# First-norm statistics as sums and centred squares on ScalarE, with the groups of three engines reordered

## The reference

```
mod = silu(c) @ wmod                      # six rows per batch: sa, ca, ga, sb, cb, gb
h   = layernorm(x) * (1 + ca) + sa        # THE FIRST NORM: mean and variance over 512 channels
z   = layernorm(h) * gamma + beta         # second norm, inside the attention block
k, v, r = z @ Wk, z @ Wv, z @ Wr
wkv = tf * kv + td * (decayed running sum of kv over the tokens before)
x   = x + ga * ((sigmoid(r) * wkv) @ Wo)
h   = layernorm(x) * (1 + cb) + sb        # third norm
x   = x + gb * (moe0(h) + moe1(h)) / 2    # two groups of 32 experts, top 2, SwiGLU, dropless
```

## Time and profile before

| | |
|---|---|
| runs | 4863.53, 4865.57, 4850.79 us |
| the profiled execution's own time | 4859.97 us |
| its span, first to last instruction | 4858.2 us |
| PE busy over the span | 4561.6 us (94%) |
| DVE busy | 3056.9 us (63%) |
| ACT busy | 1655.1 us (34%) |
| POOL busy | 2856.0 us (59%) |
| mean granted TensorE clock | 0.974 |

### The profile page before, as it was taken

How to read it: one execution, slowest core, us unless ns; L and a number is a source line. 1 busy time by engine, 2 the same in 40 slices (tenths; PEclk the granted TensorE clock), 3 DMA queues, 4 the chain that set the end, 5 groups by cost and what they waited for, 6 DMA issues and landing times.

```text
span 4858.2 us, 89097 instructions
## 1 busy us (share of the span) xinstructions
PE 4561.6 (94%) x22649; PEld 3757.8 (77%) x22649; DVE 3056.9 (63%) x6077; ACT 1655.1 (34%) x4221; POOL 2856.0 (59%) x2303
## 2 busy tenths in 40 slices
PE   6999999999999993989999998999999999999998
PEld 4878778787878773877777777888788888888886
DVE  5999999999999994444444444544344444444443
ACT  2445444444444441322222222332222222222222
POOL 2677777777777775444545454555455555555554
PEclk8999999999999996999999999999999999999999
DMA  6767676766767676899999989998998988998887
GB/s 242 237 202 241 200 227 207 219 218 210 230 200 223 203 231 206 231 285 255 260 284 269 286 243 285 273 291 201 296 243 233 248 232 229 266 239 222 210 216 193
DMA packets 434618, 1152.40 MB, mean 237 GB/s; under 512 B 59362, under 2 KB 59363, under 8 KB 415667
## 3 DMA queue, kind: packets, MB, share of 16 engines
q0 software_dynamic: 182512, 454.27, 40.3%
q1 hardware_dynamic: 231106, 619.79, 37.7%
q10 hardware_dynamic: 20736, 75.51, 4.2%
HBM read 719.35 MB, written 463.57 MB: 243 GB/s over the span
## 4 chain that ended last, share of the span: by engine, by line
PE 45%; DMA 11%; issue 3%; POOL 1%; DVE 1%; POOLq 0%; SPq 0%; DVEq 0%; ACT 0%
PE ps L1321 13%; PE ps L1323 13%; PE ps L1322 13%; DMA out<-c_yo,c_idx 10%; PE ps L1330 4%; PE ps L1349 2%; DMA c_wt<-wsp_d 1%; POOL out L1312 1%; POOL c_xg L1279 0%; DVE c_yo L1576 0%; POOL list_d L1284 0%; POOLq L1304 0%; DMA list_d<-pairs,sidx 0%; DMA c_lists<-list_d,c_rowu 0%; DVE c_xl L1564 0%
## 5 line engine op out<-in xcount | busy, mean ns | idle before, releaser
L1312 POOL DMA_INDIRECT out<-c_yo,c_idx x576 | 914.8, 1588 | 928.3 <-DMA out<-c_yo,c_idx 475.9
L1321 PE MATMUL ps<-c_wt,c_xh 128*128 128x512 f32 x2304 | 965.6, 419 | 22.6 <-issue 15.1
L1323 PE MATMUL ps<-c_wt,c_xl 128*128 128x512 f32 x2304 | 910.7, 395 | 0.0
L1322 PE MATMUL ps<-c_wt,c_xh 128*128 128x512 f32 x2304 | 904.8, 393 | 0.0
L1279 POOL DMA_INDIRECT c_xg<-h2g_d,c_idx x576 | 566.4, 983 | 519.8 <-DVE c_yo L1576 413.5
L1560 DVE TENSOR_TENSOR c_hh<-ps,c_sil 128x256 f32<-128x256 f32 x576 | 244.4, 424 | 913.7 <-ACT c_sil L1403 849.0
L1576 DVE SCALAR_TENSOR_TENSOR c_yo<-ps,c_wc,c_xg 128x512 f32<-128x512 f32 x576 | 432.5, 751 | 538.7 <-DMA out<-c_yo,c_idx 266.5
L1408 ACT CAST c_xh<-ps 128x512 fp32r<-128x512 f32 x576 | 339.3, 589 | 972.9 <-PE ps L1330 911.7
L711 POOL DMA_INDIRECT list_d<-pairs,sidx x496 | 547.6, 1104 | 186.1 <-issue 124.8
L444 PE MATMUL ps<-xTh,wTh 128*128 128x512 f32 x1536 | 621.5, 405 | 34.5 <-DVE xTl L820 16.8
L1403 ACT ACTIVATE c_sil<-ps 128x256 f32<-128x256 f32 x576 | 221.5, 384 | 1175.2 <-PE ps L1323 1125.0
(11 more groups left out here) (203 smaller groups left out, 7753.4 us busy)
## 6 DMA issues: line engine op xcount, KB each, us to landing
c_wt<-wsp_d SPq DMA_DIRECT2D x69, 2048.0 KB
sraw<-wex SPq DMA_DIRECT2D x290, 256.0 KB
wsp_d<-shigh SPq DMA_DIRECT2D x288, 256.0 KB
wsp_d<-sraw SPq DMA_DIRECT2D x288, 256.0 KB
c_wt<-wsp_d SPq DMA_DIRECT2D x69, 1024.0 KB
xin<-x SPq DMA_DIRECT2D x34, 1024.0 KB
h2g_d<-mod_d SPq DMA_DIRECT2D x128, 256.0 KB
out<-xin SPq DMA_DIRECT2D x32, 1024.0 KB
```

Source lines behind the costliest of these rows:

```text
L1312: nc.gpsimd.indirect_dma_start(out=out, out_offset=bass.IndirectOffsetOnAxis(ap=idx[:, n:n + 1], axis=0), in_=yo[:, n % 4, :], in_offset=N ...
L1321: nc.tensor.matmul(o, lh, rh, start=first, stop=False)
L1322: nc.tensor.matmul(o, lh, rl, start=False, stop=False)
L1323: return nc.tensor.matmul(o, ll, rh, start=False, stop=last)
```

## The change

The DVE statistics of the first norm leave the steps (they stay for the first two tiles, which are done before the loop). ACT computes them instead, in three new groups:

- `sums`: for each of the four j, an Identity activation over 512 channels with an accumulator output, giving the sum. The full-size output goes to a junk buffer, for which `hit` (a buffer of the router code) is lent.
- `mean`: one small Copy that scales the four sums by -1/512 into `fnm`.
- `squares`: for each j, a Square activation with bias `fnm` and an accumulator output, giving the centred sum of squares. A last small activation scales by 1/512 and adds epsilon into `vaf`.

Each of these activations waits for the one before it, since all share the junk buffer. DVE's part 1 adds `fnm` instead of subtracting the mean. The lent buffer brings waits between `sums` and DVE's `place`, and between `squares` and DVE's `topk`. Besides that the order of calls in the step functions of ACT, POOL and DVE is changed. The core of the diff:

```diff
@@ stage_out on SP: the same wait, written through gate()
-                wait(sp, low_of(j), lows(b, j))
+                gate(sp, (low_of(j), lows(b, j)))
@@ ACT, new groups
+            def sums(b, s, js):
+                u = (s + 2) % 4
+                junk = hit[:].rearrange("p k r e -> p (k r e)")
+                if js[0] == 0:
+                    n = (s + 2) // 4 + 1
+                    act.wait_ge(x_in[u], 16 * (b + n) if isinstance(b, int) else b * 16 + n * 16)
+                    wait(act, f_mean, cnt(b, s - 1, 1, 1))
+                    wait(act, at_sum, cnt(b, s - 2, 1, 1))
...
+                for j in js:
+                    wait(act, f_sq, cnt(b, s - 1, 4, 4))
+                    wait(act, f_sum, cnt(b, s, 4, j))
+                    nc.scalar.activation(junk, xin[:, u, j, :], ACT.Identity,
+                                         accum_out=fsum[:, j:j + 1]).then_inc(f_sum, 1)
+
+            def mean(b, s):
+                act.wait_ge(f_sum, cnt(b, s, 4, 4))
+                wait(act, f_sq, cnt(b, s - 1, 4, 4))
+                wait(act, h_half, cnt(b, s + 1, 4, 4))
+                nc.scalar.activation(fnm[:], fsum[:], ACT.Copy, scale=-1.0 / C).then_inc(f_mean, 1)
+
+            def squares(b, s, js):
...
+                for j in js:
+                    act.wait_ge(f_mean, cnt(b, s, 1, 1))
+                    wait(act, f_var, cnt(b, s + 1, 1, 1))
+                    wait(act, f_sq, cnt(b, s, 4, j))
+                    nc.scalar.activation(junk, xin[:, u, j, :], ACT.Square, bias=fnm[:, j:j + 1],
+                                         accum_out=fsq[:, j:j + 1]).then_inc(f_sq, 1)
+                if js[-1] == TJ - 1:
+                    act.wait_ge(f_sq, cnt(b, s, 4, 4))
+                    wait(act, f_rstd, cnt(b, s + 1, 1, 1))
+                    nc.scalar.activation(vaf[:], fsq[:], ACT.Identity, bias=epsc[:], scale=1.0 / C).then_inc(f_var, 1)
@@ ACT step, second half (the first half is in the order rows below)
                 normed(b, s)
-                stage_hi(b, at + 4)
-                chunk_k(b, s, 1)
+                chunk_k(b, s, 2)
                 stage_hi(b, at + 5)
-                chunk_r(b, s, 1)
-                chunk_k(b, s, 2)
+                squares(b, s, (2, 3))
+                stage_hi(b, at + 6)
                 if back_too:
                     turned(b, s)
+                chunk_k(b, s, 3)
                 hi(b, s, 1)
-                stage_hi(b, at + 6)
                 chunk_r(b, s, 2)
-                chunk_k(b, s, 3)
+                stage_hi(b, at + 7)
+                front(b, s, (0, 1))
+                stage_hi(b, at + 8)
+                front(b, s, (2, 3))
+                chunk_r(b, s, 3)
                 hi(b, s, 2)
-                stage_hi(b, at + 7)
-                stage_hi(b, at + 8)
                 stage_hi(b, at + 9)
-                front(b, s, (0, 1))
-                chunk_r(b, s, 3)
-                front(b, s, (2, 3))
                 hi(b, s, 3)
@@ POOL step, around rstd of the third norm
                 stage_lo(b, at + 2)
-                stage_lo(b, at + 3)
                 if not (first and s == 0):
                     rstd(b_var, vab, h2_ready, rsb, b_rstd, b, s - 1)
+                stage_lo(b, at + 3)
                 if old:
-                    scatter(b, s - 2, 0, 7)
+                    scatter(b, s - 2, 0, 6)
+                lo(b, s, 0)
...
@@ DVE, norm_front part 1
+                               scalar=mvf[:, j, 0:1] if early else fnm[:, j:j + 1], in1=mod[:, CA1, :],
+                               op0=ALU.subtract if early else ALU.add, op1=ALU.mult).then_inc(h_half, 1)
@@ DVE, topk, before it writes hit
+                    wait(dve, f_sq, cnt(b, s + 1, 4, 4))
@@ DVE step
-                norm_front(b, s + 1, 3)
                 if not (first and s < 2):
                     place(b, s - 2)
+                norm_front(b, s + 1, 3)
                 if not (first and s == 0):
                     modulate(b, s - 1)
+                chunk(b, s, 1)
+                chunk(b, s, 2)
                 stage_lo(b, s * PER_STEP + 4)
-                chunk(b, s, 1)
                 stage_lo(b, s * PER_STEP + 5)
-                chunk(b, s, 2)
                 stage_lo(b, s * PER_STEP + 6)
-                norm_front(b, s + 2, 0)
                 chunk(b, s, 3)
```

More of the change, by code:

```diff
@@ L260, in stage_a @@
         f_stats, f_aggr, f_var = sem("f_stats"), sem("f_aggr"), sem("f_var")
+        f_sum, f_mean, f_sq = sem("f_sum"), sem("f_mean"), sem("f_sq")
         h_half, h_ready = sem("h_half"), sem("h_ready")
@@ L620, in step @@
                 at = s * PER_STEP
+                stage_hi(b, at)
                 chunk_k(b, s, 0)
-                stage_hi(b, at)
                 stage_hi(b, at + 1)
@@ L626, in step @@
                     soften(b, s - 2)
+                chunk_r(b, s, 1)
+                stage_hi(b, at + 2)
                 hi(b, s, 0)
-                stage_hi(b, at + 2)
                 stage_hi(b, at + 3)
+                chunk_k(b, s, 1)
+                sums(b, s, (0, 1))
+                sums(b, s, (2, 3))
+                mean(b, s)
+                squares(b, s, (0, 1))
+                stage_hi(b, at + 4)
                 normed(b, s)
-                stage_hi(b, at + 4)
-                chunk_k(b, s, 1)
+                chunk_k(b, s, 2)
                 stage_hi(b, at + 5)
-                chunk_r(b, s, 1)
-                chunk_k(b, s, 2)
+                squares(b, s, (2, 3))
+                stage_hi(b, at + 6)
                 if back_too:
                     turned(b, s)
+                chunk_k(b, s, 3)
                 hi(b, s, 1)
-                stage_hi(b, at + 6)
                 chunk_r(b, s, 2)
-                chunk_k(b, s, 3)
+                stage_hi(b, at + 7)
[3 more added lines that the diff above has]
+                chunk_r(b, s, 3)
                 hi(b, s, 2)
-                stage_hi(b, at + 7)
-                stage_hi(b, at + 8)
                 stage_hi(b, at + 9)
-                front(b, s, (0, 1))
-                chunk_r(b, s, 3)
-                front(b, s, (2, 3))
                 hi(b, s, 3)
@@ L717, in step @@
                 at = s * PER_STEP
+                if not (first and s < 3):
+                    scatter(b, s - 3, 11, 13)
                 rstd(f_var, vaf, h_ready, rsf, f_rstd, b, s + 1)
+                stage_lo(b, at)
                 if not (first and s < 3):
-                    scatter(b, s - 3, 11, 16)
-                stage_lo(b, at)
+                    scatter(b, s - 3, 13, 15)
                 receive(b, s, 0)
                 stage_lo(b, at + 1)
-                lo(b, s, 0)
+                if not (first and s < 3):
+                    scatter(b, s - 3, 15, 16)
                 rstd(g_var, vag, z_ready, rsg, g_rstd, b, s + 1)
                 stage_lo(b, at + 2)
-                stage_lo(b, at + 3)
                 if not (first and s == 0):
                     rstd(b_var, vab, h2_ready, rsb, b_rstd, b, s - 1)
+                stage_lo(b, at + 3)
                 if old:
-                    scatter(b, s - 2, 0, 7)
+                    scatter(b, s - 2, 0, 6)
+                lo(b, s, 0)
+                if old:
+                    scatter(b, s - 2, 6, 8)
                 receive(b, s, 1)
                 if old:
-                    scatter(b, s - 2, 7, 8)
+                    scatter(b, s - 2, 8, 9)
                 lo(b, s, 1)
+                stage_lo(b, at + 7)
+                if old:
+                    scatter(b, s - 2, 9, 10)
                 receive(b, s, 2)
-                if old:
-                    scatter(b, s - 2, 8, 9)
-                lo(b, s, 2)
-                stage_lo(b, at + 7)
                 stage_lo(b, at + 8)
                 if old:
-                    scatter(b, s - 2, 9, 10)
+                    scatter(b, s - 2, 10, 11)
+                receive(b, s, 3)
                 stage_lo(b, at + 9)
-                receive(b, s, 3)
-                if old:
-                    scatter(b, s - 2, 10, 11)
+                lo(b, s, 2)
                 lo(b, s, 3)
@@ L904, in topk @@
                 wait(dve, at_sum, cnt(b, s - 1, 1, 1))
-                if isinstance(b, int) and b == 0 and s == 0:
-                    dve.wait_ge(zeroed, 96)
+                if not (isinstance(b, int) and b == B and s == -1):
+                    wait(dve, f_sq, cnt(b, s + 1, 4, 4))
                 V.tensor_tensor(hit[:], iota[:].unsqueeze(1).unsqueeze(1).to_broadcast([P, 2, R, E]),
@@ L1039, in _ @@
             g.memset(half[:], -0.5)
+            g.memset(A["epsc"][:], EPS)
             for t in (A["mvf"], A["mvg"], A["mvb"]):
```

10 lines of the change are left out of this document (8 added, 2 removed).

## The result

The changed kernel is slower: 4984.59 us (median of four runs, 4977.53 to 4997.03) against 4860.98 for the kernel before (4850.79 to 4865.57), a ratio of 1.0263 with an interval of 1.0245 to 1.0282. The forecast was 4924. The profiled execution took 4997.03 with a span of 4995.3, 137 us more than the one before it.

A forecast was written before the change was run, and what follows sets the result against it. It took PE's second third of `project` 3, waiting for DVE's chunk 2 scan, to set stage A's step. Waits 51 plus clock 22 less 9 gave 64 us on 4859.97: 4924 us, own range 4880 to 4965, whole range 4850 to 5000.

The forecast's parts named there:

- the head of ACT's new list: `chunk_r` 1 on ACT, which waits for `project` 1 to end, so the list before `chunk_k` 2 cannot begin earlier.
- 28.55: Offset in us from the step's start at which ACT's list was to begin, after `project` 1.
- 40.65: Offset where ACT's `chunk_k` 2 was to end: 28.55 plus 6.9 us of existing work and 5.2 of new activations.
- 43.6: Offset where PE's second third of `project` 3 was to begin, behind DVE's scan of chunk 2; between 42.3 and 44.5.
- first third done, with `back` hardly waiting: PE was to reach the end of `project` 3's first third at some 41.0, then stop once per step for 2.6 us.
- Waits: Later second third of `project` 3, 6.4 us per batch (51 in all), less 1.1 (9) for the wait ahead of `project` 0.
- Clock: Slow PE clock after its stop in `project` 3: half of 1.4 us per step, 22 us in all, bounds 0 and 45.
- The wait at `back` is nearly gone: Sign at PE's `back`: its wait, mostly for the scan of chunk 1, 25.0 us before, was to nearly vanish.
- The other sign: DVE was to idle before chunk 2 for ACT's `chunk_k`, PE waiting 2 to 3 us within `project` 3.
- Rival 1: On ACT, accumulating activations are cheap and no clock is lost: no change, 4860 us; chance 0.14.
- rival 3: DVE's relief decides if ACT's list does not gate chunk 2: faster, 4775 us, or 4818 for half; chance 0.14.
- Rival 2: Late `stage_lo` 4 holds the staging ring, so `front` 2 and 3 come late and `project` 0 stalls: 5004 us; chance 0.18.

The follow-up runs named there:

- Experiment 2: Changed kernel with the eight accumulating activations reading 4 of 512 channels: 4983.0 us, ratio 1.0258 to the kernel before.
- experiment 1: All three engines' new orders, but statistics left on DVE and nothing new on ACT: 4980.5 us, ratio 1.0257 to the kernel before.
- experiment 3: Changed kernel with `chunk_r` 1 moved from the head of ACT's list to directly behind `chunk_k` 1: 4931.1 us, ratio 1.0155 to the kernel before.
- experiment 10: experiment 3 with DVE's `stage_lo` 4 and 5 back ahead of chunks 1 and 2: 4883.2 us, ratio 1.0079 to the kernel before.
- experiment 4: Changed kernel with `topk` ahead of DVE's first pass (`norm_front` part 1): 4960.7 us, ratio 1.0203 to the kernel before.
- experiment 6: Kernel before with DVE's new order alone, its statistics kept on DVE: 4912.5 us, ratio 1.0132 to the kernel before.
- experiment 12: 11 with DVE's chunk 1 ahead of `stage_lo` 4: 4833.9 us, ratio 0.9970 to the kernel before.
- 8: Kernel before, all orders kept, with the statistics on ACT where it waited: 4860.8 us, ratio 1.0028 to the kernel before.
- 11: 8 with `front` moved ahead of `stage_hi` 8 and 9 on ACT, POOL rearranged accordingly: 4838.9 us, ratio 0.9981 to the kernel before.

## Why the prediction was right or wrong

**The direction was right, the place was wrong.** Slower was forecast at 0.72, and the head of ACT's new list was named for it. That 4984.59 lies above the forecast's own 4880 to 4965 but inside the whole range, 4850 to 5000, is luck: the upper end came from bounds on other terms. The head of the list does wait for `project` 1: `chunk_r` 1 starts at 866.41, offset 28.3 against the 28.55 used. ACT's list then went almost as worked out. The timeline of ACT after:

```profile
870.40 0.63 ACT L634 ACTIVATE hit<-xin 128x512 f32<-128x512 f32 x1 [1.07 <-issue]
870.94 0.18 ACT L634 ACTIVATION_READ_ACCUMULATOR hit<-xin 128x1 f32 x1
871.22 0.63 ACT L634 ACTIVATE hit<-xin 128x512 f32<-128x512 f32 x1
...
878.91 0.67 ACT L554 ACTIVATE aa<-ps,bias 128x512 f32<-128x512 f32 x1
```

The pitch of a sum is 0.82 (0.80 taken), of a square 0.93 (0.88 taken), and `chunk_k` 2 ends at 879.58, offset 41.5 against 40.65. The 0.8 between them is less than the 1.07 us ahead of the first sum. The profile calls these "issue", but `sums` wait for the reduction in `place`, which DVE ended at 870.25:

```profile
869.56 0.69 DVE L985 TENSOR_REDUCE slf<-hit 128x16 f32<-128x512 f32 x1
```

The same 0.16 us lie between the end of L985 and the first sum in all 13 of these waits above 0.3 us from 400 to 1500 us. The prediction had this wait at nothing, with `place` done before ACT arrives at 31; it was done at 32.2, since DVE was late by then through the same collisions (in the step of the kernel before, the reduction, L932, ended at 27.2). But PE did not stop for the scan behind it. DVE ended that scan at 883.55:

```profile
882.27 1.28 DVE L893 TENSOR_TENSOR_SCAN cs<-ones,cs,ps 128x512 f32<-128x512 f32 x1
```

PE reached its second third only at 885.53, offset 47.4 instead of 43.6, because it had been held up at `back` before. Experiment 2 shows that the list's length did not matter at this place, and experiment 1 that the statistics did not.

**The step that failed** is "first third done, with `back` hardly waiting". It rested on the thought that DVE's work ahead of `modulate` was unchanged, since nothing was added there. I followed the instructions that move, and not those beside which they come to lie. Three things of the order made `modulate` late, by 6 us in the step of the timeline. PE then stopped at `back` for 65.2 us by `modulate` alone, where the forecast had hardly a wait. `chunk_r` 1 at the head of ACT's list delays `stage_hi` 2, hence POOL, which then collides with `place`: experiment 3 takes that out, worth some 52 us. The late `stage_lo` delay the staging loads, hence `front`, `split_x` and the start of the first pass: experiment 10 takes two of them out, worth another 37 or so. And POOL's tail now runs beside the first pass (992 ns to 1899). That is shown as a mechanism by experiment 4, where the pass falls to 761 ns. Its price is not shown, because that kernel puts a new wait in its place; in experiment 10, with the pass at 1881 ns and PE hardly waiting for `modulate`, 0.8% is all that is left of the loss for it and everything else. The prediction mentioned POOL's late tail, for `project` 0 only.

**The mis-sized terms.** Waits: 6.4 - 1.1 = 5.3 us per batch were forecast, 8.75 measured. Clock: 0.7 per step, 2.8 per batch, were forecast, and 9.6 measured. So the clock is two thirds of what was missing. The half of 1.4 per step came from a wait ahead of `project`. The wait came ahead of the transposes of `back` instead, and in the step of the timeline they cost 1.94 more and the start of `project` 3 1.04. The bound given, 45 us in all, was too low as well: 8 x 9.6 is 77. The statistics taken from DVE were 2.9 us per step, not 3.4; the sum did not use them.

**What was to be seen.** ACT is busy for 32 to 33 us in three of the four steps, as said; DVE is not at 49 but above 53, which fits the collisions. "The wait at `back` is nearly gone" was the test, and it failed. The other sign failed too: from 400 to 1500 us DVE never idled ahead of its chunk 2. It waited 18.8 us for a `chunk_k`, six times, and each time ahead of chunk 3, behind the three `stage_lo`. Stage C is unchanged: PE is busy for 0.939 of it in both (2832.6 of 3018 us from 1840 to 4858 before, 2902 of 3090 from 1900 to 4990 after).

**The rivals.** Rival 1, no change, and rival 3, faster, both fell, but not by what stood against them: the list behind `project` 1 decided nothing. Rival 2 put the stall at `project` 0, and in the kernel after PE waits there for `split_x` only 2.8 us in all from 200 to 1600 us. But its mechanism is the nearest to what happened. DVE's order alone costs 1.3% by it (experiment 6). In the kernel after it runs as well: ACT's new order keeps `front` 2 and 3 behind `stage_hi` 8, and in the step of the timeline that cast came at 896.18, offset 58.1, later than the long end of 57.4. (The terms given for it add up to 51.9 and 56.4, not to 53 and 57.4.) Its cost shows up at `back` instead, because the late `split_x` makes DVE's first pass late (experiment 10). Rival 3's core, that DVE's relief is worth something, holds only if the order lets it through: 0.3% in experiment 12, nothing in 8.

**Open:** what the collision in the first pass costs by itself, since 4 was combined neither with 3 nor with 10; whether the 52 and 37 us would be the same taken out in the other order; and POOL's order by itself.

## What to carry to other kernels

When an order changes, write down for each engine not only what moved but what now runs beside what: an instruction that nobody touched can take twice as long beside another engine's. On an in-order engine, look first at the call whose input comes last, and list everything behind it on that engine and on the engines that wait for it; here one such call was worth 5%. Work moved off a nearly full engine gained nothing here until the next wait in line was removed too (experiments 8 and 11), and a stall of PE cost its own length and then the slow clock behind it. When one delay is found, look for a kernel that keeps it and loses the stall all the same: experiment 10 was that kernel.
